# Last attention layer of a fused transformer: value products moved to the end of a step, with the copies and the residual behind them

## What is computed

```python
xn = _layernorm(x, gamma, beta)
q = (xn @ w_q).reshape(B, SQ, 16, 64)
k, v = jnp.split(context @ w_kv, 2, axis=-1)        # each reshaped to 16 heads of 64
scores = jnp.einsum('bqhd,bkhd->bhqk', q * SCALE, k)
attn = jax.nn.softmax(scores, axis=-1)
out = jnp.einsum('bhqk,bkhd->bqhd', attn, v).reshape(B, SQ, INNER)
x = x + tanh(g_xattn[3]) * (out @ w_out + b_out) * tanh(gate[0])
```

## Time and profile before

| | |
|---|---|
| median of 3 runs | 1576.9 us (1576.74 to 1579.59) |
| span of the profiled execution | 1593.7 us |
| TensorE busy | 1390.0 us (87%) |
| VectorE busy | 1102.3 us (69%) |
| ScalarE busy | 1016.4 us (64%) |
| GpSimd busy | 533.7 us (33%) |

### The profile page before, as it was taken

How to read it: one execution, slowest core, us unless ns; L and a number is a source line. 1 busy time by engine, 2 the same in 40 slices (tenths; PEclk the granted TensorE clock), 3 DMA queues, 4 the chain that set the end, 5 groups by cost and what they waited for, 6 DMA issues and landing times.

```text
span 1593.7 us, 35101 instructions
## 1 busy us (share of the span) xinstructions
PE 1390.0 (87%) x9982; PEld 1034.7 (65%) x9982; DVE 1102.3 (69%) x3531; ACT 1016.4 (64%) x2931; POOL 533.7 (33%) x631
## 2 busy tenths in 40 slices
PE   4788887998898987998999989999986299999994
PEld 3566665676644465443666666666665299999994
DVE  4788877787777666884567767777675556666665
ACT  2688886554555564224887867877864277777762
POOL 3353566222211411000002242342243445554550
PEclk9999999999999999999999999999998599999998
DMA  8000059400499910000000010010034122222227
GB/s 194 24 8 7 14 93 178 69 0 14 96 179 179 136 34 21 0 0 7 1 8 23 13 36 18 18 34 11 18 133 156 37 62 66 67 66 65 63 57 264
DMA packets 143417, 98.35 MB, mean 62 GB/s; under 512 B 20595, under 2 KB 132510, under 8 KB 142150
## 3 DMA queue, kind: packets, MB, share of 16 engines
q1 hardware_dynamic: 134598, 80.08, 25.2%
q0 software_dynamic: 8704, 16.87, 3.2%
HBM read 43.03 MB, written 54.93 MB: 61 GB/s over the span
## 4 chain that ended last, share of the span: by engine, by line
PE 59%; DVE 13%; ACT 12%; issue 11%; another core or an unknown queue 2%; DMA 1%; DVEq 1%; SPq 1%; POOL 0%; ACTq 0%; POOLq 0%
PE bank L1450 7%; PE bank L1442 7%; PE bank L1006 6%; PE bank L1022 4%; ACT arena L1483 3%; PE bank L947 3%; PE bank L1294 3%; PE bank L1057 3%; ACT att L1620 3%; PE bank L1010 2%; PE bank L1042 2%; ACT att L1485 2%; PE bank L1032 2%; PE bank L1370 2%
## 5 line engine op out<-in xcount | busy, mean ns | idle before, releaser
L1483 ACT ACTIVATE arena<-bank 128x512 f32<-128x512 f32 (+7 forms) x380 | 245.6, 675 | 150.4 <-PE bank L1357 53.9
L1902 ACT ACTIVATE att<-bank,arena 128x128 f32<-128x128 f32 x576 | 165.0, 371 | 70.0 <-PE bank L1442 65.8
L820 POOL DMA_INDIRECT expert_outputs<-arena x144 | 145.1, 1007 | 146.6 <-issue 100.8
L1620 ACT ACTIVATE att<-bank,arena 128x128 f32<-128x128 f32 x512 | 180.7, 395 | 17.1 <-DVE arena L2160 14.6
L774 POOL DMA_INDIRECT dispatched_rows<-arena x112 | 113.8, 1016 | 181.2 <-DVE arena L2049 115.3
L608 POOL TENSOR_TENSOR ve<-mv,eps 128x4 f32<-128x4 f32 x64 | 13.0, 203 | 425.9 <-DVE mv L1965 416.9
L1450 PE MATMUL bank<-arena,att 128*128 128x128 f32 x1152 | 153.5, 276 | 2.3 <-ACT att L1902 1.7
L1442 PE MATMUL bank<-xnT,arena 128*128 128x128 f32 x1152 | 154.0, 277 | 0.4 <-ACT xnT L1483 0.4
L1450 PEld LDWEIGHTS bank<-arena,att 128*128 128x128 f32 x1152 | 140.1, 192 | 4.8 <-ACT att L1902 4.8
L1442 PEld LDWEIGHTS bank<-xnT,arena 128*128 128x128 f32 x1152 | 141.6, 194 | 1.0 <-ACT xnT L1483 1.0
L1483 ACT ACTIVATE xnT<-bank 128x128 f32<-128x128 f32 (+1 forms) x180 | 63.5, 353 | 90.9 <-PE bank L841 43.1
(11 more groups left out here) (375 smaller groups left out, 3257.0 us busy)
## 6 DMA issues: line engine op xcount, KB each, us to landing
dispatched_rows<-padf SPq DMA_DIRECT2D x16, 2128.5 KB, 31.8
arena<-dispatched_rows SPq DMA_DIRECT2D x144, 64.5 KB
cxT<-in_ctx SPq DMA_DIRECT2D x32, 256.0 KB
arena<-in_L_ffn_w SPq DMA_DIRECT2D x8, 1024.0 KB
arena<-expert_outputs SPq DMA_DIRECT2D x8, 1024.0 KB, 13.8
expert_outputs<-arena POOLq DMA_INDIRECT x144
out_x<-x SPq DMA_DIRECT2D x8, 256.0 KB, 4.9
dispatched_rows<-arena POOLq DMA_INDIRECT x112
```

The lines of the kernel that those rows point to most:

```text
L820: pl.indirect_dma_start(sent_out, bass.IndirectOffsetOnAxis(xtu3[:, s, P:P + 1], 0), yt3[:, s, :], None, bounds_check=TOP3 * TOKENS - 1, o ...
L1483: copy = lambda o, i: nc.scalar.activation(o, i, ACT.Copy)
L1620: last = nc.scalar.activation(ex3_of(w, side)[:, i, :], bank[side][:, i * P:i * P + P], ACT.Exp, bias=nm3[:, w % 2, h:h + 1], accum_out=su ...
L1902: last = nc.scalar.activation(h3[:, s % 2, k * P:k * P + P], bank[s % 2][:, k * P:k * P + P], ACT.Gelu, bias=b1c3[:, s % 4, k:k + 1])
```

## The change

TensorE: pieces two and three of a step move ahead of the project; the value products of step w - 2 move from behind the project to the end of the step, behind a fourth piece. In the drain they keep their place. VectorE: the copy of the value products (three steps late now, w - 3) moves right behind the maxima; residual and routing step 6 move from behind the maxima of step 2 to the end of step 2. In the drain, the copies of values 5 and 6 stand in its first step and that of 7 in its second.

```diff
@@ TensorE, heads3, body @@
                         for s in mine[:1]:
                             piece(c + 1, 1 - p, s)
+                        for s in mine[1:3]:
+                            piece(c + 1, 1 - p, s)
                         if w % 2 == 0 and (live and w >= 4):
                             project(c, (w - 4) // 2)
                         if w % 2 == 0 and (not first and w < 4):
                             project(c - 1, (w - 4) % PAIRS // 2)
-                        if (live and w >= 2) or (not first and w < 2):
-                            values(c, p if w >= 2 else 1 - p, w - 2)
-                        for s in mine[1:3]:
-                            piece(c + 1, 1 - p, s)
+                        if not live and w < 2:
+                            values(c, 1 - p, w - 2)
...
                             probs_T(c, w - 1)
                         for s in mine[3:]:
                             piece(c + 1, 1 - p, s)
+                        if live and (w >= 2 or not first):
+                            values(c, p if w >= 2 else 1 - p, w - 2)
@@ VectorE, heads3, body @@
                             maxima(c, w)
-                        if w == 2 and not first and live:
-                            residual(c - 1)
+                        if live and (w >= 3 or not first):
+                            values(c, w - 3)
                         if live and not more:
-                            for u in {2: (6,), 3: (7, 8), 5: (9, 10), 6: (12,)}.get(w, ()):
+                            for u in {3: (7, 8), 5: (9, 10), 6: (12,)}.get(w, ()):
                                 routing(c - 1, u)
...
                         if not live:
-                            if w < 2:
-                                values(c, w - 2)
+                            for u in {0: (-3, -2), 1: (-1,)}.get(w, ()):
+                                values(c, u)
...
-                            for u in {2: (6,), 3: (7,), 4: (8,), 5: (9,), 6: (10,), 7: (12,)}.get(w, ()):
+                            for u in {3: (7,), 4: (8,), 5: (9,), 6: (10,), 7: (12,)}.get(w, ()):
                                 routing(c - 1, u)
-                        if (live and w >= 2) or (not first and w < 2):
-                            values(c, w - 2)
-                        if live:
-                            normal(c, w, 0)
+                        normal(c, w, 0)
                         if more and ahead and 3 <= w < 7:
                             front(c + 2, w - 3)
-                        if live:
-                            normal(c, w, 1)
+                        normal(c, w, 1)
+                        if w == 2 and not first:
+                            residual(c - 1)
+                            routing(c - 1, 6)
```

## The result

| | before | after |
|---|---|---|
| median of the timed runs, 5 each | 1579.6 us (1576.7 to 1580.5) | 1609.7 us (1608.3 to 1609.8) |
| span of a profiled execution | 1575.0 us (second one) | 1607.4 us |
| mean granted clock | 0.965 | 0.957 |

The changed kernel takes 1.019 times as long (95% interval 1.018 to 1.020): 30.1 us slower. Forecast were 25, at 1602, counted from the 1576.9 us of the first three runs of before.

A forecast was written before the change was run, and what follows sets the result against it. TensorE, running its list strictly in order, was taken to set the pace, with waits deciding the last chunk. Terms 7.8 + 8.2 + 2 - 2 + 6 + 3 = +25.0 on 1576.9 gave 1602 us; range 1583 to 1617.

The forecast's parts named there:

- (a): Step 0 of chunks 1 to 6: piece 2, moved up, waits 1.0 to 1.9 us for xnT; +7.8 us.
- (b): Step 5 of 7 chunks, step 2 of chunk 0: fourth piece waits for its bank, 1.02 each; +8.2 us.
- The third piece: Needs the first piece's bank, free at 2.85, arrives at 3.02: taken as nothing, +5 us if missed.
- (c): VectorE's later residual and routing delay step 3's row normalisation, so its transposes wait about 0.3 in 6 chunks; +2 us.
- (d): VectorE's copy no longer waits 5.02 us in step 0 for a remote releaser; -2 us, bounds 0 and -6.
- (e): Last chunk, no pieces: projects wait 2.0 us for VectorE's copy in even steps, step 0's swallowed by the pause; +6 us.
- (f): TensorE's granted clock falls after idle around step 0, counted in two chunks of 8; +3 us, bounds 0 and +14.
- the lower clock follows each new wait: Rival: slow matmuls, 1.7 us, behind most new waits, +14 in place of 3; +36, 1613 us; chance 0.17.
- Old waits: Rival: new waits fall into existing ones, in step 0 and the last chunk, no clock lost; +10, 1587 us; chance 0.15.
- Faster: Rival: VectorE is freed, normals come earlier, waits ahead of scores and in the drain shrink; -12, 1565 us; chance 0.08.

The follow-up runs named there:

- second one: The kernel before, unchanged, run again for a second trace: measured 1576.9 us, span 1575.0 us.

## Why the prediction was right, and where its sizes were not

The sign, the range and most of the named mechanisms held: TensorE sets the pace, the order exposes waits, nothing is won by VectorE. The terms:

- **(a) xnT in step 0, +7.8.** The wait is there in all six chunks, at 0.87 (four) and 0.96 (two), just under the 1.0 that the earlier of the two readings gave. The later reading, 3.45, was from a chunk of the disturbed execution; xnT is ready after 2.56 to 2.57 otherwise, so waits alone are 5.4, in place of 7.8. Undone it gives 8.2 (6.8 by the ratios), as behind the turn the wait costs 2 to 3.5. About right in sum, by luck: the reading was too long and the clock behind the turn was left out.
- **(b) Fourth piece, +8.2.** Step 5 is 8.26 where 8.27 was worked out, the piece starts at 6.18 for 6.19, and there are eight such waits, where the rows had them. Undone it gives back 5.8 only, since the swapped order costs 0.47 a chunk in steps 2 and 6. The third piece was a tie, as taken.
- **(c) Residual, +2.** Step 3 is 0.24 longer, L852 starting 4.16 after the scores where 4.2 was worked out; in six chunks this is 1.4. It takes the copy ahead of the normalisation as well, as the working had it: with the residual alone step 3 keeps its 6.40.
- **(d) The pause, -2.** The remote waits were one execution's. There was nothing to win, which the prediction named as possible, and gave too little weight: the profiled span stood 16.8 over the median, and that was the sign. For the same reason the profiled execution after is 1607.4 and not 1619.
- **(e) Last chunk, +6, and (f) the clock, +3.** This is the step that failed: the last chunk's waits were counted three times and not four, and the clock behind them was all but left out. The waits ahead of the projects are 2.22, 1.97, 2.06 and 1.97, each where and as long as forecast. But step 0's was struck out, on the strength of (d); the value products then wait for the copy as well (1.04, one bank), and routing's products L863 wait 1.6 longer, as the value products no longer stand ahead of them (1.0) and VectorE's copy now does (0.6); both were not in the sum. And the clock was counted at two places in 8 chunks, from one row at full speed behind 1.47 of idle. The same rows show a project of 3.30 us behind a wait of 3.10, against 1.95 in the earlier trace rows; it was read as a wait only. With four waits of 2 us in 58 it fell to 0.82, which costs 5.4 in this pair of traces, and by some 3 us more or less in others. In total 14.7 in place of 6 plus a part of 3.
- **Not forecast: the loop's turn.** Chunks 2 and 3 pay 7.3 in place of 3.7: about 0.9 in a longer stop, the rest in slow matmuls behind it. It was not in the sum, though the trace that the prediction was read from has the stop as well: step 0 of chunk 3 is 11.99 long in it, and 11.95 in the second.

The rivals: *the lower clock follows each new wait* was right for the last chunk and behind the turn, where it costs some 8 us in the traces of before and after, and wrong in the other full chunks, where the pieces behind a wait of 0.87 or 1.28 take 1.12. *Old waits* failed, nothing swallowed a new one. *Faster* failed as argued: its condition, xnT by 1.6, did not hold, and 44 us less waiting of VectorE won nothing.

Left open: why the stop at the turn is 5.0 to 6.0 us in all nine kernels whose TensorE order was changed, by the pieces, by the products or by both, and 3.8 to 4.6 in the four traces with the old order, though TensorE has the same 9982 matmuls. The profile says "issue" and no run here varied the loop alone. The Trainium skill (Runtime: NRT & Kernel Launch, Instruction fetch mechanics) says that a taken branch whose target is not among the pages held ready stalls the engine until that page has been fetched. That would fit a stop at the loop's head; it gives no size and doesn't tell the orders apart, and no run here shows the fetch. Open too is what makes the clock fall behind one wait and not behind an equal one.

## What to carry to other kernels

When a product moves to just in front of the next dependent burst, add up for each consumer what stands between it and its copy, and do it again for the iterations that lack the filler work: here the last chunk of eight held nearly half of the loss, and moving one copy ahead of two reductions gave most of it back. Waiting of an engine that is not the bound is not a prize: 44 us of it vanished for nothing, while 0.78 us at the head of a chunk, on TensorE, was worth an edit. And before a trace is read for small waits, compare its span with the median of the runs: 16.8 us too much meant waits that were in no other execution. The reverse holds as well: where runs of one kernel spread over 8 us, a difference of 3 us between two traces need not be the edit's, and parts of the code that both kernels share show how much is not.

## What the hardware showed that was not expected

- The granted clock fell to 0.82 over 58 us in which TensorE was busy 39.67 us and no idle time was over 5.5. Filling four 2 us waits with useless products brought it to 0.91, saved 3.7 us in those steps and made the whole kernel 6.7 us faster.
- The same list of matmuls with the same waits got a clock of 0.92 in one trace and 0.85 in another (34.3 and 37.3 us for 360 matmuls): behind the same wait of 1.79 us a project took 2.05 us in the one and 3.45 in the other.
- The same wait of 0.87 us cost 0.87 in a full chunk at full clock and 2 to 3.5 behind the stop at the loop's turn, where after's clock was 0.57 over 15 us.
- Both kernels stop at the one backward turn of TensorE's loop, idle for 4.6 and 5.5 us in two parts (with the 0.8 of every chunk's head), one of them in the middle of 16 scores.
